# One reciprocal-root step for four blocks of rows in the first normalisation of a fused GNN and mixture-of-experts kernel

## The chip, the core and the metric

The kernel runs on one core of a Trainium2 chip. The metric is the device time of one execution in microseconds (us), the median of several runs. Engines are named as in the profile: PE is TensorE (PEld its weight loads), DVE is VectorE, ACT is ScalarE, POOL is GpSimd, and SP issues most of the DMA transfers.

## What is computed

`x` is 8192 rows of 128, `adj` is an 8192 by 8192 matrix. The reference, cut to what matters here:

```python
def _layernorm(x, axis=-1, eps=1e-05):
    m = jnp.mean(x, axis=axis, keepdims=True)
    v = jnp.var(x, axis=axis, keepdims=True)
    return (x - m) / jnp.sqrt(v + eps)

# first layer, z = _layernorm(x)
    msg = z @ W + B
    sens = jnp.exp(-(1.0 / r - 1.0) ** 2 / (2.0 * 0.5 * 0.5))      # r = adj
    weights = jnp.where(adj < 1.0, sens, 0.0)
    x = x + weights @ msg
# second layer, on _layernorm(x): a gate picks 2 of 16 experts for each row,
# their two-layer networks are mixed, and a last normalisation follows
    x = x + ffn(_layernorm(x))
```

The change concerns the first normalisation alone, the one that makes `z` and with it `msg`.

## The kernel before

**Tiling.** The rows are worked in 16 groups (`GROUPS`) of 512, a group being four tiles of 128 rows (`TB` = 4). For each group of output rows the kernel walks over the 8192 columns of `adj` in 16 chunks of 512 columns (`JC`), 1 MB each, which lie in a ring of eight slots (`RING`). A chunk is passed through four elementwise steps in place: `mask` (DVE), `log` and `invert` (ACT), `square` (DVE). Then it is worked in two halves (k = 0 and 1): PE turns a half by eight transposes into `tp`, ACT makes the weights of it (`weigh`, tile `wT`), and PE multiplies them with `msg` into `acc` (`products`).

**Order.** Every engine has a program of its own, written out by hand, and works strictly along it; the engines meet at semaphores. `mask` runs four chunks ahead of PE, `log` and `invert` three, `square` two. The column steps are numbered `m`, with chunk `c` and half `k`.

**The first group (g = 0)** carries extra work, because `msg` for the rows of chunk `c` must exist before PE reaches that chunk. `msg` is made block by block (a block is 512 rows, one for each chunk), two blocks of it ahead of the loop and block `c + 2` within chunk `c`:

- PE turns the rows of `x` into the bank `misc` (`message_turn`), ACT copies them to `yT` (`keep_turned`), PE multiplies them by the weights (`message_products`), and DVE scales each row by its reciprocal root `rstd` and adds the bias (`keep_messages`, four instructions, writing `msg`). The mean needs no subtraction, since the weights are centred beforehand.
- DVE takes the statistics of a block (`norm_stats`: `bn_stats` and `bn_aggr`, four each, into `mv_now`). ACT makes a first value of the reciprocal root from the variance, Exp(-0.5 Ln(v + eps)) (`guess`, two instructions, tiles `lnv` and `rs`). DVE improves it by one Newton step of four short instructions (`refine`, called by `norm_rows`, tiles `nt` and `rstd`), each waiting for the one before it.

Within chunk `c` DVE therefore runs `mask`, `norm_stats(c + 3)`, `square`, `norm_rows(c + 2)`, `keep_messages(c + 2)`; ACT runs `weigh`, `log`, `guess(c + 3)`, `weigh`, `keep_turned(c + 2)`, `invert`. From group 1 on DVE carries the second layer's gate in these places (`gate_slot`), and after the sixteenth group come the experts.

`x` arrives in four parts of 1 MB (semaphores `x_part`), each four blocks long, and each is waited for by the first block of it.

Of the kernel before, what the change touches and what calls it, by code (L numbers as in the profile page):

```python
# [18 lines left out]
def gnn_moe_kernel(nc, x, adj, gnn_w, gnn_b, gate_w, gate_b, w1, b1, w2, b2, gamma, beta, out):  # L19
# [52 lines left out]
    with ctx:  # L72
        def sb(name, shape, dt=F32):
            return ctx.enter_context(nc.sbuf_tensor(name, shape, dt))

        def sem(name):
            return ctx.enter_context(nc.semaphore(name))
# [27 lines left out]
        rstd = sb("rstd", [P, N // P])  # L105
        lnv = sb("lnv", [P, 2, TB])
        nt = sb("nt", [P, TB])
        shift = sb("shift", [P, 2, TB])
        rs = sb("rs", [P, 2, TB])
        spread = sb("spread", [P, TB])  # L110
# [84 lines left out]
        vec = sem("vector_step")  # L195
        mv_ready = sem("mv_ready")
        lnv_ready = sem("lnv_ready")
        spread_ready = sem("spread_ready")
        guessed = sem("guessed")
        rs_ready = sem("rs_ready")  # L200
# [276 lines left out]
        @block.scalar  # L477
        def _(act):
            act.preload_act_table_set("natural_log_exp_and_others")
            act.sem_inc(weighted, WSLOTS)  # L480
            act.wait_ge(const_ok, CONSTS)

            def slot(c):
                return chunk[:, c % RING, :, :]

            def log(g, c):

                act.wait_ge(masked, g * CHUNKS + c + 1)
                act.activation(slot(c), slot(c), ACT.Ln, bias=TINY).then_inc(logged, 1)  # L489

            def invert(g, c):

                act.wait_ge(logged, g * CHUNKS + c + 1)
                act.activation(slot(c), slot(c), ACT.Exp, scale=-1.0).then_inc(inverted, 1)  # L494

            def weigh(g, m):

                act.wait_ge(turned, g * PPG + m + 1)
                act.wait_ge(added, g * PPG + m + 1)
                act.activation(wT[:, (g * PPG + m) % WSLOTS, :], tp[(g * PPG + m) % TSLOTS][:, :], ACT.Exp, scale=-2.0).then_inc(weighted, 1)  # L500

            def guess(j, i, nth):


                act.wait_ge(mv_ready, j + 1)
                act.activation(lnv[:, i, :], mv_now[:, i, :, 1], ACT.Ln, bias=eps[:, 0:1]).then_inc(lnv_ready, 1)  # L506
                act.wait_ge(lnv_ready, nth + 1)
                act.activation(rs[:, i, :], lnv[:, i, :], ACT.Exp, scale=-0.5).then_inc(guessed, 1)

            def gate_slot(g, m):  # L510
                if m == 16:
                    act.wait_ge(diff_ready, g + 1)
                    act.activation(ed[:, :], dv[:, :], ACT.Exp).then_inc(exp_ready, 1)

            def keep_turned(j):

                act.wait_ge(misc_full, j * SETUP_MISC + 1)
                act.activation(yT[:, :], misc[:, :], ACT.Copy).then_inc(misc_read, 1)

            log(0, 0)  # L520
            guess(0, 0, 0)
            keep_turned(0)
            invert(0, 0)
            guess(1, 1, 1)
            log(0, 1)
            invert(0, 1)
            keep_turned(1)
            log(0, 2)
            guess(2, 0, 2)
            invert(0, 2)  # L530
            for g in range(GROUPS):
                for m in range(PPG):
                    c, k = divmod(m, PAIRS)
                    weigh(g, m)
                    if g == 0 and k == 1 and c + 2 < GROUPS:
                        keep_turned(c + 2)

                    n = c + LOG_LEAD
                    if not (g == GROUPS - 1 and n >= CHUNKS):
                        (log if k == 0 else invert)(g + n // CHUNKS, n % CHUNKS)  # L540
                    if g:
                        gate_slot(g - 1, m - BEHIND)
                    elif k == 0 and c + 3 < GROUPS:

                        guess(c + 3, (c + 3) % 2, c + 3)

            def copy_rows(u):

                act.wait_ge(rin_turned, u + 1)
                if u >= RT:  # L550
                    act.wait_ge(hid_full, u - RT + 1)
                n = UR[batch_of(u)]
                act.activation(rT[u % RT][:, 0:n], t_bank[u % T_BANKS][:, 0:n], ACT.Copy).then_inc(rT_ready, 1)  # L553

            def relu_hidden(u):

                act.wait_ge(hid_full, u + 1)
                if u >= HT:
                    act.wait_ge(o_full, u - HT + 1)
                n = UR[batch_of(u)]  # L560
                for t in range(FT):
                    ins = act.activation(hT[u % HT][:, t * n:(t + 1) * n], h_bank[u % H_BANKS][:, t * n:(t + 1) * n],  # L562
                                         ACT.Relu, bias=slots[u % SLOTS][:, B1 + t:B1 + t + 1])
                ins.then_inc(hT_ready, 1)

            def combine_slot(g, m):
                i = g % 2
                if m == 4:
                    guess(2 * GROUPS + g, i, GROUPS + g)
                if m == 7:  # L570

                    act.wait_ge(rs_ready, g + 1)
                    for b in range(TB):
                        ins = act.activation(zs[g % ZS][:, b, :], zs[g % ZS][:, b, :], ACT.Identity,
                                             bias=shift[:, i, b:b + 1], scale=rs[:, i, b:b + 1])
                    ins.then_inc(zn_ready, 1)

            for u in range(TURN_LEAD):
                copy_rows(u)
            for u in range(HIDDEN_LEAD):  # L580
                relu_hidden(u)
            for i in range(LAST):
                if i + TURN_LEAD < NU:
                    copy_rows(i + TURN_LEAD)
                if i + HIDDEN_LEAD < NU:
                    relu_hidden(i + HIDDEN_LEAD)
                if i % GATE_PACE == 0:
                    gate_slot(GROUPS - 1, i // GATE_PACE)
                for g in range(GROUPS):
                    combine_slot(g, i - starts[g])  # L590

        @block.vector
        def _(dve):
# [36 lines left out]
            def row_moments(i):  # L630
# [3 lines left out]
                    ins = dve.bn_aggr(mv_now[:, i, b, :], stats[:, b, :])  # L634
                ins.then_inc(mv_ready, 1)

            def refine(j, i, to):


                dve.wait_ge(guessed, j + 1)  # L640
                need()
                link(dve.scalar_tensor_tensor(out=nt[:, :], in0=mv_now[:, i, :, 1], scalar=EPS, in1=rs[:, i, :],
                                              op0=ALU.add, op1=ALU.mult))
                link(dve.tensor_tensor(nt[:, :], nt[:, :], rs[:, i, :], ALU.mult))
                link(dve.tensor_scalar(nt[:, :], nt[:, :], -0.5, 1.5, ALU.mult, ALU.add))
                done(dve.tensor_tensor(to, rs[:, i, :], nt[:, :], ALU.mult))
# [14 lines left out]
            def norm_stats(j):  # L661
                dve.wait_ge(x_part[j // PARTS_OF], 16)
                if j:
                    dve.wait_ge(mv_ready, j)
                row_stats(rows(xs, j))
                row_moments(j % 2)

            def norm_rows(j):
                refine(j, j % 2, rows(rstd, j))

            def keep_messages(j):

                dve.wait_ge(misc_full, j * SETUP_MISC + 2)
                need()
                for b in range(TB):
                    ins = dve.scalar_tensor_tensor(out=rows(msg, j)[:, b, :], in0=misc[:, b * D:(b + 1) * D],
                                                   scalar=rows(rstd, j)[:, b:b + 1], in1=bg_bc[:, :],
                                                   op0=ALU.mult, op1=ALU.add)
                ins.then_inc(misc_read, 1)

            def message_slot(m):

                c, k = divmod(m, PAIRS)
                if k == 0 and c + 3 < GROUPS:
                    norm_stats(c + 3)
                if k == 1 and c + 2 < GROUPS:
                    norm_rows(c + 2)
                    keep_messages(c + 2)

            mask(0, 0)  # L690
            norm_stats(0)
            norm_stats(1)
            norm_rows(0)
            mask(0, 1)
            norm_rows(1)
            square(0, 0)
            keep_messages(0)
            mask(0, 2)
            norm_stats(2)
            square(0, 1)  # L700
            keep_messages(1)
            mask(0, 3)
# [6 lines left out]
            def gate_slot(g, m):  # L709
# [9 lines left out]
                    row_stats(rows(xs, g))  # L719
                    row_moments(0)  # L720
                if m == 6:
                    refine(GROUPS + g, 0, rs[:, 0, :])
                    need()

                    dve.wait_ge(scattered, g * KB * 16)
# [212 lines left out]
            def combine_slot(g, m):  # L938
# [17 lines left out]
                if m == 3:  # L956
                    row_moments(i)
                if m == 5:
                    refine(2 * GROUPS + g, i, rs[:, i, :])
                if m == 6:  # L960
                    need()
                    dve.scalar_tensor_tensor(out=shift[:, i, :], in0=mv_now[:, i, :, 0], scalar=-1.0, in1=rs[:, i, :],
# [217 lines left out]
```

## Time and profile before

| | before |
|---|---|
| median of 3 runs | 1747.53 us (1747.34 to 1747.88) |
| the profiled execution, its own time | 1747.3 us |
| its span in the trace | 1745.6 us |
| PE busy | 1613.7 us (92%) |
| ACT busy | 1572.2 us (90%) |
| DVE busy | 1498.2 us (86%) |
| POOL busy | 508.4 us (29%) |
| DMA | 341.26 MB, mean 196 GB/s |

The span is the profiled execution from its first instruction to its last; 1.7 us of the execution's own time lie around it. A busy share is a mean over stages that differ: the first group, the fifteen others, and the experts behind them.

### The profile page before, as it was taken

Reading aid. Unit: us, or ns where it says so; the run is one execution under the profiler, and the core shown is the slowest. Engines: PE = TensorE matmul, PEld = TensorE weight load, DVE = VectorE, ACT = ScalarE, POOL = GpSimd, SP = SyncE. Lnnn points to the kernel's source line nnn. Section 1 sums busy time; section 2 is a strip of 40 time slices with the busy share of each in tenths; the row PEclk is TensorE's granted clock in tenths of the full one; section 3 lists DMA queues with packets and bytes.
Section 4 is the critical chain, followed back from the end, with each engine's and each line's share of the span. In section 5 each row is a group of like instructions: output and inputs, shape, how many; then the busy total and the mean of one; then the engine's idle time right before and its main releaser. Section 6 shows DMA issues by size and latency. Waiting matters only on the chain.

```text
span 1745.6 us, 23549 instructions
## 1 busy us (share of the span) xinstructions
PE 1613.7 (92%) x8141; PEld 1070.9 (61%) x8141; DVE 1498.2 (86%) x2272; ACT 1572.2 (90%) x1536; POOL 508.4 (29%) x342
## 2 busy tenths in 40 slices
PE   4889999999999999999899999999999999999940
PEld 3556656666666565656566666665656557999830
DVE  7999989899999999999898989899999993446776
ACT  5889999999999999999989999999999995566752
POOL 0001040504040404041505050505050602107775
PEclk9999999999999999999999999999999999999975
DMA  9447876767666666666867666667676842448653
GB/s 321 147 137 252 249 210 197 215 196 218 195 210 197 207 200 204 201 203 201 234 178 218 197 209 199 207 198 211 194 212 194 232 119 79 150 137 238 201 159 94
DMA packets 206725, 341.26 MB, mean 196 GB/s; under 512 B 17216, under 2 KB 64064, under 8 KB 206480
## 3 DMA queue, kind: packets, MB, share of 16 engines
q1 hardware_dynamic: 198288, 322.64, 62.2%
q0 software_dynamic: 8320, 17.12, 3.2%
q8 instruction: 67, 1.10, 0.3%
q14 instruction: 50, 0.41, 0.1%
HBM read 304.05 MB, written 35.65 MB: 195 GB/s over the span
## 4 chain that ended last, share of the span: by engine, by line
PE 59%; DVE 20%; POOL 8%; ACT 7%; issue 5%; DMA 1%; POOLq 0%; SPq 0%; ACTq 0%; DVEq 0%
PE acc L1060 34%; PE tp L1079 17%; DVE chunk L615 7%; POOL chunk L473 7%; DVE chunk L621 6%; PE tp L1109 2%; ACT chunk L489 2%; ACT wT L500 2%; ACT chunk L494 2%; DVE stats L627 1%; PE tp L1137 1%; PE acc L1137 1%; POOL spread L443 1%; PE misc L1012 1%; DVE y L728 1%
## 5 line engine op out<-in xcount | busy, mean ns | idle before, releaser
L1060 PE MATMUL acc<-wT,msg 128*128 128x512 f32 x2048 | 969.0, 596 | 0.0
L500 ACT ACTIVATE wT<-tp 128x1024 f32<-128x1024 f32 x512 | 784.0, 1531 | 22.9 <-PE tp L1079 22.8
L621 DVE SCALAR_TENSOR_TENSOR chunk<-chunk 128x2048 f32<-128x2048 f32 x256 | 584.9, 2285 | 67.7 <-ACT chunk L494 67.0
L489 ACT ACTIVATE chunk<-chunk 128x2048 f32<-128x2048 f32 x256 | 620.4, 2424 | 11.9 <-DVE chunk L615 11.9
L494 ACT ACTIVATE chunk<-chunk 128x2048 f32<-128x2048 f32 x256 | 622.1, 2430 | 0.0
L1079 PEld LDWEIGHTS tp<-ident,chunk 128*128 128x128 f32 x4096 | 480.4, 142 | 223.1 <-issue 211.1
L615 DVE SCALAR_TENSOR_TENSOR chunk<-chunk 128x2048 f32<-128x2048 f32 x256 | 583.8, 2281 | 2.3 <-DMA chunk<-in_adj_dram 2.3
L1079 PE MATMUL tp<-ident,chunk 128*128 128x128 f32 x4096 | 534.7, 274 | 0.0
L1060 PEld LDWEIGHTS acc<-wT,msg 128*128 128x128 f32 x2048 | 350.4, 191 | 251.8 <-issue 247.4
L455 POOL DMA_INDIRECT rows_in<-y,row_now x128 | 283.0, 2211 | 45.4 <-issue 45.4
L436 POOL TENSOR_TENSOR pool_carrier<-pool_carrier 1x1 f32<-1x1 f32 x32 | 8.4, 264 | 747.1 <-DVE row_now L792 706.6
L443 POOL TENSOR_SCALAR spread<-mv_now 128x4 f32<-128x4 f32 x16 | 45.2, 2826 | 392.8 <-DVE mv_now L634 392.8
L473 POOL DMA_INDIRECT chunk<-rows_out,row_back x128 | 126.5, 988 | 36.9 <-issue 34.9
L562 ACT ACTIVATE msg<-tp,chunk 128x256 f32<-128x256 f32 (+1 forms) x234 | 91.5, 443 | 41.9 <-PE tp L1109 41.5
L1109 PE MATMUL tp<-msg,chunk 128*128 128x256 f32 (+1 forms) x468 | 107.3, 352 | 0.0
L1109 PEld LDWEIGHTS tp<-msg,chunk 128*128 128x128 f32 x468 | 75.1, 191 | 4.5
L553 ACT ACTIVATE msg<-tp 128x256 f32<-128x256 f32 (+1 forms) x117 | 41.2, 354 | 28.5 <-PE tp L1098 28.5
L1137 PE MATMUL tp<-blobs,msg 128*128 x408 | 56.0, 277 | 3.5 <-DVE chunk L933 2.0
L1137 PEld LDWEIGHTS tp<-blobs,msg 128*128 128x128 f32 x408 | 53.4, 191 | 7.4 <-issue 5.2
L1137 PE MATMUL acc<-blobs,msg 128*128 x404 | 55.3, 277 | 1.6 <-ACT msg L562 0.7
L506 ACT ACTIVATE lnv<-mv_now,eps 128x4 f32<-128x4 f32 x32 | 9.5, 296 | 52.2 <-DVE mv_now L634 51.8
L1137 PEld LDWEIGHTS acc<-blobs,msg 128*128 128x128 f32 x404 | 52.9, 191 | 5.3 <-issue 3.3
(112 smaller groups left out, 738.4 us busy)
## 6 DMA issues: line engine op xcount, KB each, us to landing
chunk<-in_adj_dram SPq DMA_DIRECT2D x256, 1024.0 KB, 5.4
chunk<-rows_in SPq DMA_DIRECT2D x86, 128.0 KB
rows_out<-chunk SPq DMA_DIRECT2D x42, 256.0 KB, 2.6
y_kept<-y SPq DMA_DIRECT2D x16, 256.0 KB, 6.1
rows_in<-zeros SPq DMA_DIRECT2D x32, 128.0 KB
chunk<-y_kept SPq DMA_DIRECT2D x16, 256.0 KB, 3.9
out_dram<-chunk SPq DMA_DIRECT2D x16, 256.0 KB, 2.7
rows_out<-chunk SPq DMA_DIRECT2D x17, 128.0 KB, 2.2
```

The source lines that it names most:

```text
L455: pool.indirect_dma_start(rows_in, bass.IndirectOffsetOnAxis(row_now[:, k, b:b + 1].bitcast(U32), 0), y[:, b, :], None).then_inc(scattered ...
L473: pool.indirect_dma_start(back[g % BACK][:, kb, :], None, rows_out[b], bass.IndirectOffsetOnAxis(row_back[:, g, kb:kb + 1].bitcast(U32), 0 ...
L489: act.activation(slot(c), slot(c), ACT.Ln, bias=TINY).then_inc(logged, 1)
L494: act.activation(slot(c), slot(c), ACT.Exp, scale=-1.0).then_inc(inverted, 1)
L500: act.activation(wT[:, (g * PPG + m) % WSLOTS, :], tp[(g * PPG + m) % TSLOTS][:, :], ACT.Exp, scale=-2.0).then_inc(weighted, 1)
L562: ins = act.activation(hT[u % HT][:, t * n:(t + 1) * n], h_bank[u % H_BANKS][:, t * n:(t + 1) * n], ACT.Relu, bias=slots[u % SLOTS][:, B1 ...
L615: dve.scalar_tensor_tensor(out=slot(c), in0=slot(c), scalar=1.0, in1=slot(c), op0=ALU.is_lt, op1=ALU.mult).then_inc(masked, 1)
L621: dve.scalar_tensor_tensor(out=slot(c), in0=slot(c), scalar=2.0, in1=slot(c), op0=ALU.subtract, op1=ALU.mult).then_inc(squared, 1)
L1060: ins = pe.matmul(acc[:, :], msg[:, n, :], wT[:, (g * PPG + m) % WSLOTS, k * ROWS:(k + 1) * ROWS], start=(n == 0), stop=(n == 2 * PPG - 1))
L1079: ins = pe.transpose(tp[s % TSLOTS][:, t * ROWS + b * P:t * ROWS + (b + 1) * P], chunk[:, c % RING, b, j:j + P], ident[:, :])
L1109: ins = pe.matmul(h_bank[u % H_BANKS][:, t * n:(t + 1) * n], slots[u % SLOTS][:, W1 + t * P:W1 + (t + 1) * P], rT[u % RT][:, 0:n], start=T ...
L1137: ins = pe.matmul(o_bank[u % O_BANKS][:, r:r + D], hT[u % HT][:, t * n + r:t * n + r + P], blobs[:, bass.ds(second_layers[u], 1), W2 + t * ...
```

## The change

- The statistics of a block go to a new tile `mv_part`, which holds four blocks and is kept twice (`part_moments`).
- ACT makes the first value of the root for four blocks in one go (`guess_part`, two instructions on 16 columns in place of two on 4 for each block). It waits for the statistics of the last of the four blocks.
- DVE improves the four blocks' values by one Newton step (`refine_part`, four instructions on 16 columns), once in four chunks. A new semaphore `normed` says that it is done; `keep_messages` and the next `guess_part` wait for it.
- The statistics run two chunks sooner: chunk `c` takes those of block `c + 5` in place of `c + 3`. Ahead of the loop five blocks are taken and not three, four of them before the second `mask`.
- Numbers of the other guesses (second and last normalisation) are renumbered, nothing else in them changes.

```diff
--- before.py
+++ after.py
@@ -105,6 +105,10 @@
         rstd = sb("rstd", [P, N // P])
         lnv = sb("lnv", [P, 2, TB])
         nt = sb("nt", [P, TB])
+        mv_part = sb("mv_part", [P, 2, PARTS_OF * TB, 2])
+        lnv_part = sb("lnv_part", [P, PARTS_OF * TB])
+        rs_part = sb("rs_part", [P, PARTS_OF * TB])
+        nt_part = sb("nt_part", [P, PARTS_OF * TB])
         shift = sb("shift", [P, 2, TB])
         rs = sb("rs", [P, 2, TB])
         spread = sb("spread", [P, TB])
@@ -195,6 +199,7 @@
         vec = sem("vector_step")
         mv_ready = sem("mv_ready")
         lnv_ready = sem("lnv_ready")
+        normed = sem("normed")
         spread_ready = sem("spread_ready")
         guessed = sem("guessed")
         rs_ready = sem("rs_ready")
@@ -517,16 +522,23 @@
                 act.wait_ge(misc_full, j * SETUP_MISC + 1)
                 act.activation(yT[:, :], misc[:, :], ACT.Copy).then_inc(misc_read, 1)
 
+            def guess_part(p):
+
+                act.wait_ge(mv_ready, (p + 1) * PARTS_OF)
+                if p:
+                    act.wait_ge(normed, p)
+                act.activation(lnv_part[:, :], mv_part[:, p % 2, :, 1], ACT.Ln, bias=eps[:, 0:1]).then_inc(lnv_ready, 1)
+                act.wait_ge(lnv_ready, p + 1)
+                act.activation(rs_part[:, :], lnv_part[:, :], ACT.Exp, scale=-0.5).then_inc(guessed, 1)
+
             log(0, 0)
-            guess(0, 0, 0)
             keep_turned(0)
             invert(0, 0)
-            guess(1, 1, 1)
+            guess_part(0)
             log(0, 1)
             invert(0, 1)
             keep_turned(1)
             log(0, 2)
-            guess(2, 0, 2)
             invert(0, 2)
             for g in range(GROUPS):
                 for m in range(PPG):
@@ -540,9 +552,9 @@
                         (log if k == 0 else invert)(g + n // CHUNKS, n % CHUNKS)
                     if g:
                         gate_slot(g - 1, m - BEHIND)
-                    elif k == 0 and c + 3 < GROUPS:
-
-                        guess(c + 3, (c + 3) % 2, c + 3)
+                    elif k == 0 and (c + 2) % PARTS_OF == 0 and c + 2 < GROUPS:
+
+                        guess_part((c + 2) // PARTS_OF)
 
             def copy_rows(u):
 
@@ -566,7 +578,7 @@
             def combine_slot(g, m):
                 i = g % 2
                 if m == 4:
-                    guess(2 * GROUPS + g, i, GROUPS + g)
+                    guess(2 * GROUPS + g, i, X_PARTS + g)
                 if m == 7:
 
                     act.wait_ge(rs_ready, g + 1)
@@ -634,6 +646,23 @@
                     ins = dve.bn_aggr(mv_now[:, i, b, :], stats[:, b, :])
                 ins.then_inc(mv_ready, 1)
 
+            def part_moments(j):
+
+                need()
+                for b in range(TB):
+                    ins = dve.bn_aggr(mv_part[:, j // PARTS_OF % 2, j % PARTS_OF * TB + b, :], stats[:, b, :])
+                ins.then_inc(mv_ready, 1)
+
+            def refine_part(p):
+
+                dve.wait_ge(guessed, p + 1)
+                link(dve.scalar_tensor_tensor(out=nt_part[:, :], in0=mv_part[:, p % 2, :, 1], scalar=EPS, in1=rs_part[:, :],
+                                              op0=ALU.add, op1=ALU.mult))
+                link(dve.tensor_tensor(nt_part[:, :], nt_part[:, :], rs_part[:, :], ALU.mult))
+                link(dve.tensor_scalar(nt_part[:, :], nt_part[:, :], -0.5, 1.5, ALU.mult, ALU.add))
+                dve.tensor_tensor(rstd[:, p * PARTS_OF * TB:(p + 1) * PARTS_OF * TB], rs_part[:, :], nt_part[:, :],
+                                  ALU.mult).then_inc(normed, 1)
+
             def refine(j, i, to):
 
 
@@ -663,15 +692,12 @@
                 if j:
                     dve.wait_ge(mv_ready, j)
                 row_stats(rows(xs, j))
-                row_moments(j % 2)
-
-            def norm_rows(j):
-                refine(j, j % 2, rows(rstd, j))
+                part_moments(j)
 
             def keep_messages(j):
 
                 dve.wait_ge(misc_full, j * SETUP_MISC + 2)
-                need()
+                dve.wait_ge(normed, j // PARTS_OF + 1)
                 for b in range(TB):
                     ins = dve.scalar_tensor_tensor(out=rows(msg, j)[:, b, :], in0=misc[:, b * D:(b + 1) * D],
                                                    scalar=rows(rstd, j)[:, b:b + 1], in1=bg_bc[:, :],
@@ -681,22 +707,22 @@
             def message_slot(m):
 
                 c, k = divmod(m, PAIRS)
-                if k == 0 and c + 3 < GROUPS:
-                    norm_stats(c + 3)
+                if k == 0 and c + 5 < GROUPS:
+                    norm_stats(c + 5)
                 if k == 1 and c + 2 < GROUPS:
-                    norm_rows(c + 2)
+                    if (c + 2) % PARTS_OF == 0:
+                        refine_part((c + 2) // PARTS_OF)
                     keep_messages(c + 2)
 
             mask(0, 0)
-            norm_stats(0)
-            norm_stats(1)
-            norm_rows(0)
+            for j in range(PARTS_OF):
+                norm_stats(j)
             mask(0, 1)
-            norm_rows(1)
             square(0, 0)
+            refine_part(0)
             keep_messages(0)
             mask(0, 2)
-            norm_stats(2)
+            norm_stats(PARTS_OF)
             square(0, 1)
             keep_messages(1)
             mask(0, 3)
@@ -719,7 +745,7 @@
                     row_stats(rows(xs, g))
                     row_moments(0)
                 if m == 6:
-                    refine(GROUPS + g, 0, rs[:, 0, :])
+                    refine(X_PARTS + g, 0, rs[:, 0, :])
                     need()
 
                     dve.wait_ge(scattered, g * KB * 16)
@@ -956,7 +982,7 @@
                 if m == 3:
                     row_moments(i)
                 if m == 5:
-                    refine(2 * GROUPS + g, i, rs[:, i, :])
+                    refine(X_PARTS + GROUPS + g, i, rs[:, i, :])
                 if m == 6:
                     need()
                     dve.scalar_tensor_tensor(out=shift[:, i, :], in0=mv_now[:, i, :, 0], scalar=-1.0, in1=rs[:, i, :],
```

The order of DVE's instructions at the start of its program, from the first `mask` on. `chunk` is a slot of the ring, `xs` holds the rows of `x`. Before:

```order
L615 SCALAR_TENSOR_TENSOR chunk<-chunk 128x2048
L627 BN_STATS stats<-xs 128x6 x4
L634 BN_AGGR mv_now<-stats 128x2 x4
L627 BN_STATS stats<-xs 128x6 x4
L634 BN_AGGR mv_now<-stats 128x2 x4
L642 SCALAR_TENSOR_TENSOR nt<-mv_now,rs 128x4
L644 TENSOR_TENSOR nt<-nt,rs 128x4
L645 TENSOR_SCALAR nt<-nt 128x4
L646 TENSOR_TENSOR rstd<-rs,nt 128x4
L615 SCALAR_TENSOR_TENSOR chunk<-chunk 128x2048
```

Of the changed kernel (its line numbers are higher by 12 or more), from the same first `mask`:

```order
L627 SCALAR_TENSOR_TENSOR chunk<-chunk 128x2048
L639 BN_STATS stats<-xs 128x6 x4
L653 BN_AGGR mv_part<-stats 128x2 x4
L639 BN_STATS stats<-xs 128x6 x4
L653 BN_AGGR mv_part<-stats 128x2 x4
L639 BN_STATS stats<-xs 128x6 x4
L653 BN_AGGR mv_part<-stats 128x2 x4
L639 BN_STATS stats<-xs 128x6 x4
L653 BN_AGGR mv_part<-stats 128x2 x4
L627 SCALAR_TENSOR_TENSOR chunk<-chunk 128x2048
L633 SCALAR_TENSOR_TENSOR chunk<-chunk 128x2048
L659 SCALAR_TENSOR_TENSOR nt_part<-mv_part,rs_part 128x16
```

The second `mask` has two more blocks of statistics ahead of it and one Newton step less; the Newton step now stands behind the first `square`.

The order of ACT's instructions in one chunk of the first group (the chunk c = 3), with the semaphores that they wait for. Before:

```order
L500 ACTIVATE wT<-tp 128x1024 [waits added,turned]
L489 ACTIVATE chunk<-chunk 128x2048 [waits masked]
L506 ACTIVATE lnv<-mv_now,eps 128x4 [waits mv_ready]
L508 ACTIVATE rs<-lnv 128x4 [waits lnv_ready]
L500 ACTIVATE wT<-tp 128x1024 [waits added,turned]
L518 ACTIVATE yT<-misc 128x512 [waits misc_full]
L494 ACTIVATE chunk<-chunk 128x2048 [waits logged]
```

Of the changed kernel, in the same chunk:

```order
L505 ACTIVATE wT<-tp 128x1024 [waits added,turned]
L494 ACTIVATE chunk<-chunk 128x2048 [waits masked]
L505 ACTIVATE wT<-tp 128x1024 [waits added,turned]
L523 ACTIVATE yT<-misc 128x512 [waits misc_full]
L499 ACTIVATE chunk<-chunk 128x2048 [waits logged]
```

The pair that waits for DVE's statistics (`mv_ready`) is gone from this chunk. It stands, 16 columns wide, in the chunks c = 2, 6 and 10 and once ahead of the loop.

## Rows read from the trace of the kernel before

**Rows 1.** Windows: us, busy time by engine, PEclk, DMA share, GB/s; two stages.

```profile
80.00:100.00 20.00, 17.13 (x93) 11.21 (x92) 18.84 (x50) 16.70 (x20) 0.00 (x0) 1.00 0.46 130
200.00:250.00 50.00, 50.00 (x237) 30.95 (x235) 43.51 (x37) 50.00 (x39) 17.58 (x9) 1.00 0.78 229
```

**Rows 2.** Timeline, DVE: start us, length us, instruction, idle before it; messages of chunks 1, 12.

```profile
46.37 1.12 DVE L676 SCALAR_TENSOR_TENSOR msg<-misc,rstd,bg_bc 128x128 f32<-128x128 f32 x4 [0.64 <-PE misc L1012]
...
131.45 1.13 DVE L676 SCALAR_TENSOR_TENSOR msg<-misc,rstd,bg_bc 128x128 f32<-128x128 f32 x4 [0.37 <-PE misc L1012]
```

**Rows 3.** Timeline of one chunk (c = 8), from its predecessor's messages to its own.

```profile
92.79 1.13 DVE L676 SCALAR_TENSOR_TENSOR msg<-misc,rstd,bg_bc 128x128 f32<-128x128 f32 x4 [0.37 <-PE misc L1012]
...
93.83 2.28 DVE L615 SCALAR_TENSOR_TENSOR chunk<-chunk 128x2048 f32<-128x2048 f32 x1
...
96.03 0.86 DVE L627 BATCH_NORM_STATS2 stats<-xs 128x6 f32<-128x128 f32 x4
...
97.22 2.26 DVE L621 SCALAR_TENSOR_TENSOR chunk<-chunk 128x2048 f32<-128x2048 f32 x1
97.34 0.30 ACT L506 ACTIVATE lnv<-mv_now,eps 128x4 f32<-128x4 f32 x1 [0.85 <-DVE mv_now L634]
...
97.78 1.00 ACT L500 ACTIVATE wT<-tp 128x1024 f32<-128x1024 f32 x1
...
98.68 0.59 ACT L518 ACTIVATE yT<-misc 128x512 f32<-128x512 f32 x1
...
99.32 1.16 PE L1012 MATMUL misc<-wgs,yT 128*128 128x128 f32 x8 [0.95 <-ACT yT L518]
99.40 0.15 DVE L642 SCALAR_TENSOR_TENSOR nt<-mv_now,rs 128x4 f32<-128x4 f32 x1
...
100.52 1.13 DVE L676 SCALAR_TENSOR_TENSOR msg<-misc,rstd,bg_bc 128x128 f32<-128x128 f32 x4 [0.37 <-PE misc L1012]
```

**Rows 4.** Timeline, PE, chunk c = 13, whose program has no statistics.

```profile
131.25 1.04 PE L1079 MATMUL tp<-ident,chunk 128*128 128x128 f32 x8
...
135.15 1.88 PE L1060 MATMUL acc<-wT,msg 128*128 128x512 f32 x4
...
136.92 1.16 PE L1012 MATMUL misc<-wgs,yT 128*128 128x128 f32 x8
...
137.91 1.04 PE L1079 MATMUL tp<-ident,chunk 128*128 128x128 f32 x8
```

**Rows 5.** Timeline of the start, ahead of the loop and in chunk 0.

```profile
12.60 0.87 DVE L627 BATCH_NORM_STATS2 stats<-xs 128x6 f32<-128x128 f32 x4 [1.66 <-DMA xs<-in_x_dram]
...
13.99 0.87 DVE L627 BATCH_NORM_STATS2 stats<-xs 128x6 f32<-128x128 f32 x4
...
15.19 0.13 DVE L642 SCALAR_TENSOR_TENSOR nt<-mv_now,rs 128x4 f32<-128x4 f32 x1
...
15.83 2.28 DVE L615 SCALAR_TENSOR_TENSOR chunk<-chunk 128x2048 f32<-128x2048 f32 x1
...
18.03 0.16 DVE L642 SCALAR_TENSOR_TENSOR nt<-mv_now,rs 128x4 f32<-128x4 f32 x1
...
18.70 2.29 DVE L621 SCALAR_TENSOR_TENSOR chunk<-chunk 128x2048 f32<-128x2048 f32 x1
...
30.86 1.91 ACT L489 ACTIVATE chunk<-chunk 128x2048 f32<-128x2048 f32 x1 [1.56 <-DVE chunk L615]
...
34.26 0.30 ACT L506 ACTIVATE lnv<-mv_now,eps 128x4 f32<-128x4 f32 x1 [1.49 <-DVE mv_now L634]
...
36.25 2.08 PE L1012 MATMUL misc<-wgs,yT 128*128 128x128 f32 x8 [6.03 <-ACT yT L518]
```

**Rows 6.** Timeline of SP; DMA issues up to 60 us: median us to landing last.

```profile
9.82 1.00 SPq L282 DMA_DIRECT2D xs<-in_x_dram  x1
...
xs<-in_x_dram SPq DMA_DIRECT2D x4, 0.5 KB, 11.7
```

**Rows 7.** Window of PE: us, PE busy, PEclk, DMA share, GB/s.

```profile
38.00:40.00 2.00, 2.00 (x11) 0.50 0.99 332
```

## The prediction

> **What bounds the kernel now.** I read the windows first. In the groups after the first, ACT is busy for all of its time and PE for all of its own, while DVE has slack; in the first group no engine is full, DVE 18.84 of 20 us, PE 17.13, ACT 16.70 [rows 1]. So in the first group the engines wait for one another in turn, and the timeline shows how. From the messages of chunk 1 at 46.37 us to those of chunk 12 at 131.45 us lie 11 chunks of 7.73 us each [rows 2]. One of them, read as a chain [rows 3]: DVE starts the messages at 92.79, masks at 93.83, takes statistics from 96.03; ACT has waited 0.85 us for these, makes its guess at 97.34, goes on to the weights at 97.78 and to the copy `yT` at 98.68; PE has waited 0.95 us for the copy and starts its products at 99.32; DVE has meanwhile squared (97.22) and refined (99.40 on), waits 0.37 us for the products and starts the next messages at 100.52. The loop is closed by a false neighbour: the copy `yT` does not need the guess, it only stands behind it on ACT. A gain here reaches the end, since everything later is a fixed program that starts earlier: after the group ACT or PE is full again, whatever the hour.
>
> **What a chunk costs without the guess.** Three own loops replace the chain.
> - PE: its instructions of one chunk laid end to end. Chunk 13 has no statistics and no guess in the old program as well; there the first transposes start at 131.25 and those of the next chunk at 137.91, thus 6.66 us, and PE waits for nothing [rows 4].
> - DVE: messages to mask 1.04, mask to statistics 2.20, statistics to square 1.19, square to what follows 2.18 (97.22 to 99.40), in sum 6.61 us [rows 3]. Gone are the wait of 0.37 and the refinement, which is the rest of the 7.73, 0.75.
> - ACT: of its 7.73 us it waits 0.85 and spends 0.44 on the guess (97.34 to 97.78) [rows 3]; at most 6.44 are left.
>
> PE is the longest, DVE 0.05 behind. In chunk 13 the copy released the products at 136.92, where PE's last products, started at 135.15, were over just before [rows 4]; so the copy holds PE up by under 0.1 there, and I take 6.66.
>
> **Where the chain stays.** In the chunks c = 2, 6 and 10 ACT still has its guess, for four blocks, behind the statistics of the block that DVE has just taken, since the fourth of a part is always the newest; and DVE refines in the same chunk. These are the same instructions in the same places as in rows 3, only with 16 columns for 4. No row has that width. Bounds: nothing more than now, and at most what the 128-column statistics take, 0.87 us for four, thus 0.22 each [rows 3], against 0.15 for the narrow one: under 0.1 each. The pair on ACT lies on the chain (at most 0.2 a chunk, three times; I take 0 since the widths are nearer to 4 than to 128), the four on DVE fit into its wait of 0.37. So these three chunks keep 7.73.
>
> **The groups of edits and the sum.** The 11 chunks c = 2 to 12 take 11 x 7.73 = 85.1 now [rows 2] and 3 x 7.73 + 8 x 6.66 = 76.5 then: 8.6 us less. Chunk 13 and those behind it are PE's and ACT's already: 0. That statistics leave the chunks 11 and 12 frees DVE only: 0 there.
>
> **The start.** Before the second mask DVE gets two more blocks of statistics, each 1.39 us (12.60 to 13.99), and loses a refinement of 0.64 (15.19 to 15.83): mask 2.14 late. Behind it a refinement of 0.67 goes (18.03 to 18.70), so the square is 1.47 late, and then one of 0.75, a little wider, comes ahead of the first messages: those and everything in DVE's order behind them are 2.3 late [rows 5]. Does it reach the chain? ACT's third-ahead `log` at 30.86 waits for DVE's mask, moves to 33.2, and the next instruction can start 1.9 later, at 35.1, as it now can at 32.8 (34.26 less the wait of 1.49). Now ACT waits 1.49 us there for the next statistics and makes a guess of 0.44, so the weights start at 34.26 + 0.44 = 34.70 [rows 3, 5]. Both go from this place; the weights start at 35.1 and the products of block 2, now at 36.25, at 36.6. Of 2.3 us about 0.4 is left. On DVE: its next square lies 2.3 late as well, but no refinement follows it of 0.75, and the rest of the delay falls into the wait for those products; the messages of block 2 come 0.3 to 0.4 late too. Through chunk 1 PE runs without a pause now and then, and the 0.4 stays. The first statistics of part 1 of `x` come at about 26.4 us; that part is issued at 9.82 and such parts land 11.7 us after their issue [rows 6], by about 22, and later parts have more room: 0. The new wait for `normed` has DVE's own earlier instruction behind it, as the old `need()` had: 0. DMAs are neither moved nor added; a chunk of 1 MB in 6.66 us needs less than the groups behind take [rows 1].
>
> The Trainium skill has a rule that speaks against batching here ("Perfetto Trace Analysis", section "Optimizing Scalar/DVE Operations"): grouping helps where the engine is full, but where an engine only makes others wait, breaking instructions up may let work finish sooner. By that rule the start loses its whole 2.3 us; the rows give 0.4, because ACT had been waiting there.
>
> **Sum.** -8.6 + 0.4 = -8.2. The profiled execution took 1747.3 us with a span of 1745.6, so 1739.1; the median shown is 0.2 above it, so about **1739.2 us** is forecast.
>
> **The rivals.**
> - *PE's clock holds through the start.* PE is idle for 6.03 us before 36.25 [rows 5], and then works at 1.2 GHz (granted clock 0.50 at 38 to 40 us) [rows 7]: products take 2.08 there and 1.16 in the loop [rows 3, 5]. In the new order PE's work ahead of the gap ends some 2.3 later, so the gap is about 4 us. If the clock stays at 2.4 GHz, DVE sets chunk 1: messages of block 2 at 38.7, of block 3 at 38.7 + 6.6 = 45.3, against 46.37 + 0.4 [rows 2]. 1.5 more: 1737.7. For it: the gap is shorter. Against: the rows don't show how short it has to be.
> - *The start's loss isn't absorbed* (the rule above as a mechanism: the first root comes 2.3 late and PE's first products with it). Then -8.6 + 2.3 = -6.3: 1741.1. For it: the first messages really are 2.3 late; against: ACT's wait of 1.49.
> - *Three nearly equal loops rub.* PE 6.66, DVE 6.61, ACT 6.44: if each of the eight chunks loses one hand-over more, such as a refining instruction costs (0.75 over four, 0.19 [rows 3]), it is 1.5: 1740.7.
> - *The stall of the three batch chunks is absorbed too*: 3 x 1.07 more, 1736.0. Against: PE's copy stands hard behind the guess.
> - *The change does nothing for the chunk*: another wait holds 7.73, for instance the weights' own wait for PE's transposes. Then +0.4: 1747.7. Against: chunk 13, where the same order ran at 6.66.
> - *Slower*: the clock stays at 1.2 GHz beyond chunk 1, because PE's first work is broken up differently. A chunk of PE then takes twice 6.66, 13.3, which is 6.7 over the forecast; from two such chunks on the gain is gone, with three it is 1739.2 + 20 = 1759. Against: now PE's clock is back within chunk 1 after a longer gap, and the loop rows are all at the fast level.
>
> **How the numbers follow.** Chances: the forecast 0.40, the clock held 0.23, loss not absorbed 0.11, rubbing 0.10, batch stall absorbed 0.05, nothing gained 0.06, slower 0.05. Faster by over 0.2% (3.5 us, about what can be told from no change) are the first five, 0.89; within 0.2% 0.06; slower 0.05. The range 1736.5 to 1742.0 takes in the first four, and with wider instructions on ACT (0.6) and rubbing together 1741.4; it leaves out the last three, 0.16.
>
> **What the new profile would show.** From chunk 3 on: the copy `yT` right behind weights, PE without a wait before its products, DVE without a refinement; messages 6.66 apart, but 7.73 apart into chunks 2, 6 and 10. ACT's wait for statistics in three chunks and at the start only. Second mask at 18.0, first messages at 23.2, products of block 2 at 36.6; the first transposes of chunk 13 near 123. The groups behind keep their length. Wrong would be: messages still 7.73 apart; a first group shorter by 8 us but a later stage longer; or products of block 2 later than 37.5, or a granted clock of 0.50 past 45 us.

## The result

The changed kernel takes 1739.83 us (median of 6 runs, 1738.45 to 1740.66) against 1747.39 us (6 runs, 1746.56 to 1747.88): 7.6 us less, ratio 0.9956 with a 95% interval of 0.9945 to 0.9967. The forecast was 1739.2 us.

The page and the windows of the changed kernel; the windows stand beside [rows 1]. Columns: busy time with count for PE, PEld, DVE, ACT and POOL, then PEclk, DMA share, GB/s.

```profile
PE 1617.0 (93%) x8141; PEld 1074.2 (62%) x8141; DVE 1491.4 (86%) x2224; ACT 1567.3 (90%) x1512; POOL 507.6 (29%) x342
```

```profile
80.00:100.00 20.00, 19.02 (x107) 13.20 (x107) 19.44 (x44) 18.43 (x16) 0.00 (x0) 1.00 0.55 163
200.00:250.00 50.00, 50.00 (x234) 30.67 (x233) 43.59 (x38) 50.00 (x38) 22.07 (x11) 1.00 0.78 234
```

In the first group PE is busy for 19.02 of 20 us in place of 17.13; in the groups behind PE and ACT are as full as before. The messages of chunks 1 and 2 and of the last one, on DVE's timeline of the changed kernel (these answer to [rows 2]; the last one is chunk 13, the messages of chunk `c` being those of block `c + 2`):

```profile
46.88 1.13 DVE L702 SCALAR_TENSOR_TENSOR msg<-misc,rstd,bg_bc 128x128 f32<-128x128 f32 x4 [1.53 <-PE misc L1038]
54.63 1.12 DVE L702 SCALAR_TENSOR_TENSOR msg<-misc,rstd,bg_bc 128x128 f32<-128x128 f32 x4 [0.34 <-PE misc L1038]
...
130.11 1.13 DVE L702 SCALAR_TENSOR_TENSOR msg<-misc,rstd,bg_bc 128x128 f32<-128x128 f32 x4 [1.13 <-PE misc L1038]
```

From those of chunk 1 on they are apart, chunk by chunk from c = 2 to 13: 7.75, 6.67, 6.66, 6.66, 7.76, 6.66, 6.66, 6.66, 7.76, 6.66, 6.67, 6.66 us. A chunk with the batch's guess and the one behind it, all engines (this answers to [rows 3]):

```profile
80.54 0.59 ACT L523 ACTIVATE yT<-misc 128x512 f32<-128x512 f32 x1
...
81.18 1.16 PE L1038 MATMUL misc<-wgs,yT 128*128 128x128 f32 x8 [0.98 <-ACT yT L523]
81.23 0.17 DVE L659 SCALAR_TENSOR_TENSOR nt_part<-mv_part,rs_part 128x16 f32<-128x16 f32 x1
...
82.38 1.13 DVE L702 SCALAR_TENSOR_TENSOR msg<-misc,rstd,bg_bc 128x128 f32<-128x128 f32 x4 [0.35 <-PE misc L1038]
...
86.28 1.02 ACT L505 ACTIVATE wT<-tp 128x1024 f32<-128x1024 f32 x1 [0.20 <-PE tp L1105]
...
87.20 0.59 ACT L523 ACTIVATE yT<-misc 128x512 f32<-128x512 f32 x1
...
87.84 1.16 PE L1038 MATMUL misc<-wgs,yT 128*128 128x128 f32 x8
...
89.04 1.13 DVE L702 SCALAR_TENSOR_TENSOR msg<-misc,rstd,bg_bc 128x128 f32<-128x128 f32 x4
```

In chunk 6 PE still waits 0.98 us for the copy; in chunk 7 the copy starts 0.92 behind the weights, PE's products follow without a wait, and DVE comes straight to its messages.

The start, on the timeline of the changed kernel: DVE's second mask and first messages, ACT's `log` and the weights behind it (this answers to [rows 5]):

```profile
17.91 2.26 DVE L627 SCALAR_TENSOR_TENSOR chunk<-chunk 128x2048 f32<-128x2048 f32 x1
...
23.21 1.12 DVE L702 SCALAR_TENSOR_TENSOR msg<-misc,rstd,bg_bc 128x128 f32<-128x128 f32 x4
```

```profile
33.17 1.91 ACT L494 ACTIVATE chunk<-chunk 128x2048 f32<-128x2048 f32 x1 [1.84 <-DVE chunk L627]
34.99 1.00 ACT L505 ACTIVATE wT<-tp 128x1024 f32<-128x1024 f32 x1
```

How the lead stands later is read from DVE's copy of the finished sum, which it makes once a group. The first and the last of the sixteen, of the old kernel and then of the changed one:

```profile
153.67 0.69 DVE L707 COPY yT<-acc 128x512 f32<-128x512 f32 x1 [3.01 <-PE acc L1060]
...
1464.74 0.69 DVE L707 COPY yT<-acc 128x512 f32<-128x512 f32 x1 [11.73 <-PE acc L1060]
```

```profile
145.66 0.69 DVE L733 COPY yT<-acc 128x512 f32<-128x512 f32 x1 [3.01 <-PE acc L1086]
...
1456.68 0.69 DVE L733 COPY yT<-acc 128x512 f32<-128x512 f32 x1 [11.32 <-PE acc L1086]
```

The lead is 8.01 us after the first group and 8.06 after the sixteenth; at the end of the span (1738.9 against 1745.6) it is 6.7. So the first group gave what it should, and in this execution 1.3 us went in the experts' stage. The traced execution is the longest of the six; by the medians the changed kernel is 7.6 us ahead, so that the usual loss is nearer to 0.5 us.

### The profile page after: what moved, and what is told of

The parts are those of the page before. It is cut to its first block, busy times and chain, and to the rows that moved or that the text cites. A ratio compares the mean times of both kernels' runs of the same rounds, so it can differ in the third digit from the quotient of the medians.

```text
span 1738.9 us, 23464 instructions
## 1 busy us (share of the span) xinstructions
PE 1617.0 (93%) x8141; PEld 1074.2 (62%) x8141; DVE 1491.4 (86%) x2224; ACT 1567.3 (90%) x1512; POOL 507.6 (29%) x342
## 4 chain that ended last, share of the span: by engine, by line
PE 66%; DVE 21%; ACT 7%; issue 3%; POOL 1%; DMA 1%; SPq 0%; DVEq 0%; ACTq 0%; POOLq 0%
PE acc L1086 35%; PE tp L1105 18%; DVE chunk L633 7%; DVE chunk L627 7%; PE tp L1135 5%; PE tp L1163 2%; PE acc L1163 2%; ACT chunk L494 2%; ACT chunk L499 2%; ACT wT L505 2%; DVE stats L639 2%; PE tp L1124 1%; DVE chunk L974 1%; POOL spread L448 1%; DVE y L754 1%
## 5 line engine op out<-in xcount | busy, mean ns | idle before, releaser
L959 DVE TENSOR_TENSOR chunk<-tp,blobs 128x256 f32<-128x256 f32 (+1 forms) x59 | 22.6, 383 | 37.8 <-PE tp L1163 37.1
```

## The experiments

"End of group 1" below is the start of that first copy: 153.67 in the old kernel, 145.66 in the changed one. It is the finest measure of what the change touches; each value is of one execution, and three executions of the changed kernel give 145.66, 144.95 and 145.09, two of the old one 153.67 and 153.86. Four of the kernels below (the first three and the first repetition of the changed one) ran on a chip on which the old kernel too takes some 110 us longer (median 1858.43 us); their traces have the group stages as elsewhere and the experts' stage longer, so these are compared by their ratios on that chip and by the end of group 1.

**The copy ahead of the guess, in the old kernel.** One call moves on ACT; no work is removed.

```diff
                     if g == 0 and k == 1 and c + 2 < GROUPS:
                         keep_turned(c + 2)
+                        if c + 3 < GROUPS:
+                            guess(c + 3, (c + 3) % 2, c + 3)
...
-                    elif k == 0 and c + 3 < GROUPS:
-                        guess(c + 3, (c + 3) % 2, c + 3)
```

> The old kernel with one line moved on ACT: the guess for block c + 3 stands behind the copy yT of block c + 2, not ahead of the second weights. No work is removed. Theory (the false neighbour closes the loop): PE no longer waits for the copy, DVE becomes the longest loop with 6.61 + 0.75 = 7.36 us a chunk against 7.73, so 11 x 0.37 = 4.1 us less, and up to 1.3 more from chunk 0: 1742 to 1743.5. Rival (only the removed refining work on DVE counts): no change, 1747.4.

Measured: ratio 0.9962 (0.9948 to 0.9977), end of group 1 at 147.97, 5.7 us sooner. Messages on its DVE timeline, of chunk 1, of chunks 7 and 8, and of chunk 12:

```profile
44.64 1.12 DVE L675 SCALAR_TENSOR_TENSOR msg<-misc,rstd,bg_bc 128x128 f32<-128x128 f32 x4
...
89.51 1.13 DVE L675 SCALAR_TENSOR_TENSOR msg<-misc,rstd,bg_bc 128x128 f32<-128x128 f32 x4
...
96.99 1.13 DVE L675 SCALAR_TENSOR_TENSOR msg<-misc,rstd,bg_bc 128x128 f32<-128x128 f32 x4
...
126.90 1.13 DVE L675 SCALAR_TENSOR_TENSOR msg<-misc,rstd,bg_bc 128x128 f32<-128x128 f32 x4
```

The two in the middle lie 7.48 apart and DVE has no wait left: it is the bound. The order on ACT alone brings 5.7 us, of the change's 8.0. But the two don't gain in the same places. Of the 5.7 us, 1.7 lie ahead of chunk 1's messages (44.64 against 46.37 [rows 2]), where the change loses 0.5; 2.8 lie in the chunks 2 to 12 (82.26 us in place of 85.08), where the change saves 8.5; and 1.2 lie behind. So in the loop the order gives 0.25 us of the 1.07 that a chunk without guess gains. The expectation was missed on both sides: 5.7 is over the 4.1 and up to 1.3, and the part in the loop is under 4.1. The chunk was forecast at 7.36; a refinement that nothing covers costs 0.87 and not 0.75, since from the start of its last instruction to the messages it takes 0.28 (89.23 to 89.51).

**No Newton step, in the old kernel.** The guess stays where it was; the first normalisation's roots are less exact here.

```diff
             def norm_rows(j):
-                refine(j, j % 2, rows(rstd, j))
+                dve.wait_ge(guessed, j + 1)
+                done(dve.tensor_copy(rows(rstd, j), rs[:, j % 2, :]))
```

> The old kernel, in which the Newton step of the first normalisation is left out: DVE copies the first value of the root in one instruction in place of four, so the roots are less exact. The guess stays ahead of the copy on ACT. Theory (the chain statistics, guess, weights, copy, products, messages sets the chunk): DVE's refining is beside the chain, its wait for the products grows from 0.37 to about 1.0, messages stay 7.73 apart, change under 0.7 us (the start). Rival (DVE is what bounds the first group, 94% busy): 12 x 0.6 = 7 us less.

Measured: ratio 0.9996 (0.9987 to 1.0006), end of group 1 at 152.92, 0.75 sooner, all of it from the start. DVE's copy and messages of one chunk:

```profile
90.91 0.16 DVE L670 COPY rstd<-rs 128x4 f32<-128x4 f32 x1
92.03 1.13 DVE L677 SCALAR_TENSOR_TENSOR msg<-misc,rstd,bg_bc 128x128 f32<-128x128 f32 x4 [0.96 <-PE misc L1013]
```

Three of four refining instructions less, and their time is found again as waiting: 0.96 in place of 0.37. Messages stay 7.73 apart. The pair settles it: as long as the guess stands ahead of the copy, DVE's refining is worth nothing in the loop (its mask and statistics stand ahead of the guess and are part of the chain); with the copy free, DVE's whole list counts. In eight of the eleven chunks the change did both, and so reached PE's 6.66. The old kernel with both edits at once was not run.

**The copy ahead of the batch's guess, in the changed kernel.**

```diff
                         keep_turned(c + 2)
+                        if (c + 2) % PARTS_OF == 0:
+                            guess_part((c + 2) // PARTS_OF)
...
-                    elif k == 0 and (c + 2) % PARTS_OF == 0 and c + 2 < GROUPS:
-                        guess_part((c + 2) // PARTS_OF)
```

> The changed kernel with the same move: the guess for four blocks stands behind the copy yT in chunks 2, 6 and 10. Theory: the stall of 1.09 us that is left in these three chunks goes; DVE has 7.45 us of work there, but PE needs the messages only about 1.2 us after they come, so PE stays at 6.66: 3 x 1.09 = 3.3 us less than the changed kernel. Rival: DVE sets these chunks with 7.45, then 3 x 0.3 = 0.9 us less.

Measured: ratio 0.9943 (0.9927 to 0.9959) beside 0.9949 of the changed kernel on the same chip, end of group 1 at 142.97 beside 144.95: 2.0 us less, between the two expectations. Messages on its DVE timeline around the third batch:

```profile
101.07 1.12 DVE L701 SCALAR_TENSOR_TENSOR msg<-misc,rstd,bg_bc 128x128 f32<-128x128 f32 x4
...
108.59 1.13 DVE L701 SCALAR_TENSOR_TENSOR msg<-misc,rstd,bg_bc 128x128 f32<-128x128 f32 x4
...
114.09 1.12 DVE L701 SCALAR_TENSOR_TENSOR msg<-misc,rstd,bg_bc 128x128 f32<-128x128 f32 x4
```

DVE now works from behind chunk 1's messages to those of chunk 10 without a pause, 7.52 us with a refinement and 6.61 without (6.76 once), falls behind PE, and makes up in chunk 11 (5.50), where it has no statistics. My slack of 1.2 us covers one batch; DVE gives back only 0.05 in each chunk between, so the second and third come out as DVE's own time. Not all of the 2.0 us lasts: at the end of group 16 this kernel is 1.2 us ahead of the changed one on the same chip (1454.81 against 1455.99).

**The unaltered kernels again.**

> The changed kernel once more, unaltered, for how its time varies. In the trace of the changed kernel the lead over the old one is 8.0 us at the end of the first group and still 8.06 at the end of the sixteenth, but 6.7 at the end of the span. Theory: the 1.3 us are lost in the experts' stage by chance (its TensorE clock fell once to 1.2 GHz there, for 3.4 us, which the old kernel's trace does not have), so this run's lead at the end of group 16 is again 8.0, and the experts' stage may take 0 to 2 us more or less. Rival: the change itself makes that stage longer; then the same 1.3 us show again.

> The old kernel, unaltered, profiled beside the others of this call. Theory: the group stages are the same to 0.1 us wherever they run (messages 7.73 apart, end of the first group at 153.7, of the sixteenth at 1464.7), and what differs between chips and executions is the experts' stage alone. Rival: the stages differ too, and then leads read inside a trace must be taken within one chip.

> The changed kernel, unaltered, once more. Its first trace lost 1.4 us of its lead between 1620 us and the end, with one fall of TensorE's clock at about 1642 us. Theory: that was chance of the execution; a second trace keeps a lead of 8.0 to 8.8 us up to the end of the sixteenth group, and its experts' stage is 0 to 1.5 us longer than the old one's. Rival: the start shifted the experts' stage for good, the same 1.4 us at the same place.

Old: end of group 1 at 153.86, of group 16 at 1464.87, 1747.38 us: the same to 0.2 us. Changed, first repetition (the chip with the long experts' stage, ratio 0.9949, 0.9934 to 0.9964): 144.95 and 1455.99. Changed, second repetition: 1740.08 us, ratio 0.9955 (0.9941 to 0.9968), 145.09 and 1456.51. In both repetitions chunk 1 took 7.44 and 7.45 where the first trace has 8.23; the rest of the group is equal to 0.02 a chunk. The first repetition can't speak on the experts' stage, which is a different one on its chip. In the second the expectation failed: its lead goes from 8.2 us at the end of group 16 to 6.8 at the end, and falls at the same place as in the first trace. Nor does every execution lose it: the six of the changed kernel took 1738.45 to 1740.66 us, the traced one is the longest, and the shortest is 8.9 us ahead of the old kernel's median. PE's windows of the two, first trace ahead (columns: PE busy, PEclk, DMA share, GB/s):

```profile
1635.00:1640.00 5.00, 5.00 (x32) 0.66 0.68 204
```

```profile
1635.00:1640.00 5.00, 5.00 (x33) 0.66 0.65 198
```

PE's first matmuls behind its pause just before, in the first trace, in the old kernel, and in the kernel of the next experiment:

```profile
1634.29 0.71 PE L1163 MATMUL tp<-blobs,msg 128*128 x4 [1.86 <-issue]
```

```profile
1641.38 0.71 PE L1137 MATMUL tp<-blobs,msg 128*128 x4 [1.25 <-ACT msg L562]
```

```profile
1631.48 0.71 PE L1166 MATMUL tp<-blobs,msg 128*128 x4 [1.69 <-issue]
```

PE stood still for 1.86 us, and then its granted clock is at 1.2 GHz for part of the stretch, 0.66 in the mean; in the old kernel the pause is 1.25 us and the clock stays up. The next kernel has a pause of 1.69 us there and no fall. Neither the three kernels below nor the old kernel, twice, have the fall at this place.

**Statistics out of the start.** The kernel with the copy ahead of the batch's guess, and:

```diff
-                if k == 0 and c + 5 < GROUPS:
+                if k == 0 and c == 0:
+                    norm_stats(4)
+                if k == 0 and c == 1:
+                    norm_stats(5)
+                    norm_stats(6)
+                if k == 0 and c > 1 and c + 5 < GROUPS:
                     norm_stats(c + 5)
...
             mask(0, 2)
-            norm_stats(PARTS_OF)
             square(0, 1)
```

> The changed kernel with the guess behind the copy, and block 4's statistics taken out of the start: chunk 0 takes block 4, chunk 1 blocks 5 and 6, from chunk 2 on block c + 5 as before. Theory (DVE works without a pause from its first statistics to chunk 0's messages, so the start is as long as DVE's list): messages of block 2 come 1.2 us sooner, chunk 1 is 1.2 us of work longer and had 0.7 us of waiting, net 0.7 us less than with the guess behind the copy alone. Rival (the start is set by PE or by the transfers): no change or 0.5 us more.

Measured: 1736.48 us, ratio 0.9934 (0.9920 to 0.9947); end of group 1 at 142.27, 0.7 less than 142.97, as expected, but no more than three executions of the changed kernel differ by; the shift of the messages is the firmer sign. Messages of blocks 0 to 3:

```profile
23.29 1.12 DVE L701 SCALAR_TENSOR_TENSOR msg<-misc,rstd,bg_bc 128x128 f32<-128x128 f32 x4
...
28.74 1.12 DVE L701 SCALAR_TENSOR_TENSOR msg<-misc,rstd,bg_bc 128x128 f32<-128x128 f32 x4
...
37.54 1.12 DVE L701 SCALAR_TENSOR_TENSOR msg<-misc,rstd,bg_bc 128x128 f32<-128x128 f32 x4
...
45.54 1.12 DVE L701 SCALAR_TENSOR_TENSOR msg<-misc,rstd,bg_bc 128x128 f32<-128x128 f32 x4
```

None waits. In the kernel without this edit blocks 2 and 3 come at 38.82 and 46.23, so here 1.28 and 0.69 us sooner; the messages of block 2 differ by 0.2 between the unaltered executions (38.65 to 38.86). The start is DVE's list, and what is taken out of it counts in full until the next pause.

**PE's clock kept up.** 64 transposes of the identity into an empty bank, whose result nobody reads; once with the copy ahead of the batch's guess, once in the changed kernel as it is.

```diff
+            def keep_warm(n):
+                for i in range(n):
+                    pe.transpose(tp[2][:, (i % 8) * P:(i % 8 + 1) * P], ident[:, :], ident[:, :])
...
                 message_products(j)
+                if j == 0:
+                    keep_warm(40)
...
                     if g == 0 and c + 2 < GROUPS:
+                        if s == 1:
+                            keep_warm(24)
```

> The changed kernel with the guess behind the copy, and 64 more transposes of the identity on PE, 40 behind the first block's products and 24 in chunk 0, into a bank that is empty then: work for nothing, in PE's two gaps of the start. Theory (chunk 1 is stretched by PE's clock of 1.2 GHz): granted clock stays at 2.4 GHz level from then on, products of block 2 take 1.16, chunk 1 becomes DVE's 6.61 us in place of 7.4 to 8.2: 0.8 to 1.6 us less than without. Rival: the clock does not hold, or the extra transposes delay PE's products: 0 to 2 us more.

> The changed kernel and nothing else altered but the 64 idle transposes in PE's two gaps of the start. It prices the rival of the prediction that PE's clock holds. Theory: messages of blocks 2 and 3 lie 6.6 apart (8.23 in the first trace of the changed kernel, 7.44 in the second), so 0.8 to 1.6 us less than the changed kernel; the stalls in chunks 2, 6 and 10 stay 7.75. Rival: chunk 1 is stretched by something else, no change.

Measured: the first 1736.29 us, ratio 0.9936 (0.9923 to 0.9950), end of group 1 at 142.00 beside 142.97; the second 1738.40 us, ratio 0.9945 (0.9932 to 0.9959), beside 1740.08 on the same chip, and 144.24 beside 145.66 and 145.09. Products of block 2 and the messages around them, in the second:

```profile
36.76 1.16 PE L1038 MATMUL misc<-wgs,yT 128*128 128x128 f32 x8
```

```profile
38.86 1.12 DVE L702 SCALAR_TENSOR_TENSOR msg<-misc,rstd,bg_bc 128x128 f32<-128x128 f32 x4
...
45.46 1.12 DVE L702 SCALAR_TENSOR_TENSOR msg<-misc,rstd,bg_bc 128x128 f32<-128x128 f32 x4
```

Chunk 1 takes 6.60, DVE's time, where the changed kernel has 8.23 or 7.45. So PE at 1.2 GHz in chunk 1 costs that kernel 0.8 to 1.6 us. In the second kernel the experts' stage kept the lead: 9.05 us at the end of group 16, 9.0 at the end of the span. So of the 1.7 us between the medians, 0.85 lie in the first group (144.24 against 145.09 on the same chip) and about as much in the experts' stage. The kernel with the statistics spread and the first of these two, both at 1736 us, are the fastest that ran on the usual chips and beat both the old and the changed kernel; between them nothing can be told. Their edits together were not tried; both take away the same wait of DVE in chunk 1, so their gains may not add up.

## Why the prediction was right, and where it was off

**The bound.** Right: the first group ran as one chain, closed by ACT's order and not by any engine's load. The pair of experiments on the old kernel shows it: the order alone gives 5.7 us, less of DVE's refining alone 0.75. What the prediction calls a false neighbour is only the first lock, though: in the loop the order alone takes a chunk to 7.48, and the rest of the way to 6.66 needs DVE's refinement gone as well.

**The chunk.** Eight chunks at 6.66, forecast 6.66; three at 7.75 to 7.76, forecast 7.73. The wide instructions took some 0.01 to 0.02 more each than the narrow ones (DVE 0.17 to 0.18 against mostly 0.15 to 0.17, ACT's pair 0.31 and 0.22 against 0.30 and 0.20). The three loops do not rub.

**The start.** Second mask at 17.91 (forecast 18.0), first messages at 23.21 (23.2), products of block 2 at 36.53 (36.6). Of the 2.3 us that the first messages come late, 0.3 are left at those of block 2 (38.65 against 38.37, from the first trace) and 0.5 at those of block 3 (46.88 against 46.37 [rows 2]), forecast 0.4; in the repetitions these come at 46.16 and 46.31, so nothing is left. The Trainium skill's rule that breaking up may let work finish sooner where an engine makes others wait ("Perfetto Trace Analysis", section "Optimizing Scalar/DVE Operations") holds for the first 23 us; the wait that the same batch removed paid for it. That DVE has no pause at all in the new start I had not said, and a block's statistics moved out of it bring block 2's messages forward by 1.28 us: 0.10 of that the first messages have already (23.29 against 23.39), and the rest is the length of the statistics, 1.20 (26.45 to 27.65).

**The sum.** Forecast 8.2; 8.01 at the end of group 1 in the first trace, of which the chunks 2 to 12 gave 8.5 (76.57 us in place of 85.08, forecast 8.6) and the start took 0.5. The repetitions have 8.72 and 8.58 (against 153.67). That the median came within 0.7 us of the forecast owes something to luck: a first group that is better than forecast in two of three traces and a loss in the experts' stage offset one another. The last steps of the prediction's arithmetic are off by 0.1 and 0.2: its own terms give 1739.3 for the forecast and 1747.9 for the rival in which nothing is gained.

**The step that was off** is "a gain here reaches the end, since everything later is a fixed program that starts earlier". It held over the fifteen groups behind the first to 0.05 us in the first trace and 0.35 in the second; two of the other kernels lose more there, the one with the copy ahead of the batch's guess 0.8 (a lead of 10.70, then 9.93) and the one with the statistics spread 0.7 (11.40, then 10.71). In the experts' stage it failed by 1.3 to 1.5 us in both traces of the changed kernel that can be compared, and by some 0.5 in its medians: a pause of PE of 1.86 us in place of 1.25, followed by a stretch at 1.2 GHz. Kernels that reach the stage 1 to 3 us sooner lose under 0.7, and the old one, 8 us later, has no such fall. That the stage's length depends on when it begins would fit these traces, one execution each; it is not shown. Why the pause is longer, and whether the clock is the whole of the loss, stays open too.

**The rivals.** "PE's clock holds", 0.23, came in half: the products of block 2 ran at 1.16 and 1.21 in the repetitions and at 2.08 in the first trace, and the clock fell behind them. Its price, 1.5, is 1.6 against the first trace. The products of block 2 in the first trace and in the two repetitions:

```profile
36.53 2.08 PE L1038 MATMUL misc<-wgs,yT 128*128 128x128 f32 x8 [2.71 <-ACT yT L523]
```

```profile
36.62 1.16 PE L1038 MATMUL misc<-wgs,yT 128*128 128x128 f32 x8 [2.72 <-ACT yT L523]
```

```profile
36.77 1.21 PE L1038 MATMUL misc<-wgs,yT 128*128 128x128 f32 x8 [4.01 <-ACT yT L523]
```

The rival asked how short the pause has to be. The rows answer that its length alone doesn't decide: with pauses of 2.71 and 2.72 us the same program came out at either level, and pauses of 4.00 to 4.01 us gave 1.21 here, 1.43 in the kernel with the statistics spread and 1.84 in the one with the copy ahead of the batch's guess. "Stall absorbed" was rightly small as a rival, but one moved call makes it real for 2.0 of 3.3 us.

## What to carry to other kernels

When engines wait in turn, follow the chain across queues before counting work: an instruction that only stands ahead of what others need can be the bound, and moving it is free, until the next engine's own list becomes the bound. Removing work from an engine that waits at the end of its list changes nothing until that order is mended. Then read each engine's own loop from a chunk that lacks the part in question: here it gave the new time to 0.01 us.

## What the runs showed of the hardware

PE's pauses at the start have a price behind them: the first blocks' eight products take 2.07 to 2.08 us and those in the loop 1.16, and with idle transposes in the pauses those of block 2 took 1.16 in both kernels that have them. The Trainium skill ("TensorE: Matmul & The Clock Gate", section "Why this matters for your kernels") advises against long idle gaps between bursts of matmuls; the runs agree, with 0.8 to 1.6 us here. The PEclk column is no safe guide in the first 40 us: in the first trace of the changed kernel it reads 1.00 while products take 2.08, in the old kernel's 0.50 [rows 7].

```profile
36.00:38.00 2.00, 1.47 (x7) 1.00 1.07 288
```

The changed kernel lost 1.3 to 1.5 us in a stage that no edit touched, at the same place in both traces that can be compared; its other executions took up to 2.2 us less, so this is no constant of the program.

One chip needs some 110 us more for the kernel, behind the sixteenth group: in the changed kernel's repetition there, that group ended at 1455.99, as elsewhere, but PE is busy for 24.51 of 50 us between 1550 and 1600 us, in the first trace for all 50. Why is open. Whole times are comparable only within one chip; the ends of the groups agree across chips to within 0.7 us for one kernel.
